# Attention outputs in tiles of 32 columns with sums of key tiles, the maxima's transfers first, the values' bias at the split

## The reference, cut to what matters

```
x = x + attn(layernorm(x))
x = x + ffn(layernorm(x))
attn: Q, K, V = x@Wq.T+bq, x@Wk.T+bk, x@Wv.T+bv; rotary Q, K
      scores = Q K^T / sqrt(32), causal;  out = softmax(scores) @ V;  out @ Wo.T + bo
ffn:  (silu((x@gate.T)*gs) * ((x@up.T)*us)) @ down.T * ds
```

## Time and profile before

| | us |
|---|---|
| median of three runs | 750.68 (748.65 to 753.9) |
| the profiled execution | 749.88 |
| its span, from the first to the last instruction | 748.2 |

### The profile page before, as it was taken

How to read it: one execution, slowest core, us unless ns; L and a number is a source line. 1 busy time by engine, 2 the same in 40 slices (tenths; PEclk the granted TensorE clock), 3 DMA queues, 4 the chain that set the end, 5 groups by cost and what they waited for, 6 DMA issues and landing times.

```text
span 748.2 us, 10633 instructions
## 1 busy us (share of the span) xinstructions
PE 732.0 (98%) x3563; PEld 539.3 (72%) x3563; DVE 443.8 (59%) x1071; ACT 310.9 (42%) x641; POOL 247.7 (33%) x224
## 2 busy tenths in 40 slices
PE   8999999999999999999999999999999999999996
PEld 7887888766656666666666548788788888888885
DVE  6978684897778787777878545853243125114113
ACT  3322231266666666666666662222332232222221
POOL 0816152411114242333324245822232223223223
PEclk9999999999999999999999999999999999999999
DMA  8686469635576667676667356540001001001001
GB/s 280 230 284 232 162 254 309 255 115 160 162 192 172 185 172 194 168 188 164 187 162 187 102 185 225 222 201 1 0 20 38 0 1 56 0 0 56 1 1 59
DMA packets 54318, 104.39 MB, mean 140 GB/s; under 512 B 14820, under 2 KB 18404, under 8 KB 53748
## 3 DMA queue, kind: packets, MB, share of 16 engines
q1 hardware_dynamic: 54264, 103.72, 44.0%
HBM read 69.62 MB, written 38.21 MB: 144 GB/s over the span
## 4 chain that ended last, share of the span: by engine, by line
PE 81%; DVE 6%; issue 5%; DMA 3%; POOL 2%; ACT 1%; SPq 1%; DVEq 0%; POOLq 0%; ACTq 0%
PE ps L1105 32%; PE ps L1244 18%; PE ps L1130 10%; PE ps L1223 10%; PE ps L1320 9%; DMA x_st<-in_x 1%; PE ps L1097 1%; POOL hid_lo L592 1%; DVE xn L786 1%; DVE stats L771 1%; DMA rec_l<-rec_rows 1%; DMA w_st<-in_wk 1%; DMA l_cols<-o_raw 1%; ACT p L683 0%; DVE esin L893 0%
## 5 line engine op out<-in xcount | busy, mean ns | idle before, releaser
L683 ACT ACTIVATE p<-ps 128x384 f32<-128x384 f32 (+3 forms) x384 | 162.0, 489 | 58.0 <-PE ps L1223 57.8
L843 DVE CUSTOM_DVE_ANT_0 masked<-ps,mask_qk 128x512 bf16<-128x512 f32 (+1 forms) x240 | 113.2, 500 | 56.6 <-PE ps L1130 55.7
L1244 PE MATMUL ps<-p,v_slot 128*64 128x512 f32 (+3 forms) x768 | 137.3, 494 | 0.2 <-ACT o_raw L690 0.2
L1223 PE MATMUL ps<-q_st,k_st 99*128 99x384 f32 (+2 forms) x384 | 135.7, 361 | 1.1 <-ACT p L683 1.0
L1056 DVE SCALAR_TENSOR_TENSOR hid<-ps,us_sb,silu 128x512 f32<-128x512 f32 x44 | 33.0, 751 | 165.2 <-PE ps L1105 159.5
L1130 PE MATMUL ps<-k_st,q_st 96*128 96x512 f32 (+2 forms) x384 | 128.9, 357 | 2.0 <-DVE row_max L843 1.7
L592 POOL TENSOR_TENSOR hid_lo<-hid,hid_hi 128x512 fp32r<-128x512 f32 x44 | 56.8, 1290 | 173.0 <-ACT hid_hi L758 173.0
L561 POOL TENSOR_SCALAR_AFFINE_SELECT p<-p 128x512 f32<-128x512 f32 x64 | 40.6, 635 | 209.0 <-ACT p L683 209.0
L1244 PEld LDWEIGHTS ps<-p,v_slot 128*64 128x64 f32 x768 | 50.1, 136 | 74.2 <-issue 62.2
L1130 PEld LDWEIGHTS ps<-k_st,q_st 96*128 96x128 f32 x384 | 72.3, 189 | 29.7 <-DVE row_max L843 14.3
L1223 PEld LDWEIGHTS ps<-q_st,k_st 99*128 99x128 f32 x384 | 72.1, 189 | 16.9 <-issue 6.3
(11 more groups left out here) (117 smaller groups left out, 1080.8 us busy)
## 6 DMA issues: line engine op xcount, KB each, us to landing
qk_scratch<-st_hi SPq DMA_DIRECT2D x32, 512.0 KB, 3.6
q_st<-qk_scratch SPq DMA_DIRECT2D x32, 384.0 KB, 3.8
k_st<-qk_scratch SPq DMA_DIRECT2D x32, 384.0 KB, 4.8
flag_st<-in_ffn SPq DMA_DIRECT2D x32, 264.0 KB, 2.8
ffn_copy<-in_ffn SPq DMA_DIRECT2D x32, 264.0 KB, 3.5
qk_scratch<-st_lo SPq DMA_DIRECT2D x16, 512.0 KB, 3.7
o_T<-o_raw SPq DMA_DIRECT2D x32, 128.0 KB, 4.2
rec_l<-rec_rows SPq DMA_DIRECT2D x32, 128.0 KB, 3.3
```

The costliest lines, as they stand in the source:

```text
L683: act.activation(p32[:, at:at + q0 + w - keep], ps[:, ST_BANK + i % ST_RING, keep - q0:w], ACT.Exp, scale=SCALE).then_inc(exp_done, 1)
L843: ins = dve.tensor_tensor_reduce((masked_a if u < 2 else masked)[:, s_before(i) % 2, col:col + kept], scores, mask_qk[:, 512 - kept:512], ...
L1223: pe.matmul(ps[:, ST_BANK + i % ST_RING, 0:w], k_st[0:K_ALL, slot, kt * P:(kt + 1) * P], q_st[0:K_ALL, slot, q0:q0 + w], start=True, stop= ...
L1244: ins = pe.matmul(ps[VW * a:VW * (a + 1), o_bank(u, half), q0 - 512 * half:512], v_slot[:, slot, kt, :], p32[:, at:at + n], start=(kt == 0 ...
```

## The change

It has these parts.

- Output products: the second half of the queries becomes two quarters (parts 1 and 2, 256 queries each). In them the values, and the rows that held the sums, are separate matmuls of 32 columns, four tiles side by side for a pair. POOL adds the probabilities of key tiles 0 to 3 (`sum_p`, heads 0 to 29), and one product with ones takes that sum. In the rows beside the sums a second set of columns ("w") takes the values' products of some key tiles; they are added later on POOL (`o_w`). The last pair has the old kind of product in quarters (`PV_TAIL`).
- ACT copies three parts out of PSUM for each pair, not two; a pair's move has six transfers, not four.
- SP's step begins with the maxima's rows; the pair's move and the reciprocals' rows come after them.
- The bias of the values is no longer added by POOL, but in `o_hi` and `o_lo`, in four pieces for each tile.
- The weights' test runs in two halves, the output weights are loaded in step 30 and not in stage A, the two small loads for stage C come ahead of the last moves, and POOL's order of the last groups changes. The reciprocals' place on DVE stays; their wait counts six transfers for a pair.

```diff
@@ -94,11 +95,33 @@
 GROUPS = HEADS // 4
 PV_AFTER = ((3, 9), (3, 9))
 TEST_AFTER = (4, 4)
-PV_GROUPS = [[(0, 0), (0, 1), (0, 2), (0, 3)], [(1, 0), (1, 1)], [(1, 2), (1, 3), (1, 7)], [(1, 4), (1, 5), (1, 6)]]
-assert len(PV_GROUPS) == len(PV_AFTER[0]) + len(PV_AFTER[1])
-assert sorted(sum(PV_GROUPS, [])) == [(0, kt) for kt in range(4)] + [(1, kt) for kt in range(KT)]
-PV_HIGH = min(g for g, group in enumerate(PV_GROUPS) if any(2 * kt >= KT for _, kt in group))
-PV_LAST = ((0, 3), PV_GROUPS[-1][-1])
+PV_GROUPS = [
+    (0, [[("vl", 0)], [("vl", 1)], [("vl", 2)], [("vl", 3)]]),
+    (1, [[("v", 0), ("w", 4)], [("v", 1), ("l", None)], [("v", 2), ("l", 4)], [("v", 3), ("l", 5)], [("w", 5)]]),
+    (2, [[("v", 0), ("w", 6)], [("v", 1), ("l", None)], [("v", 2), ("l", 4)]]),
+    (2, [[("v", 3), ("l", 5)], [("v", 4), ("l", 6)], [("v", 5), ("l", 7)], [("w", 7)]]),
+]
+PV_TAIL = [
+    PV_GROUPS[0],
+    (1, [[("vl", kt)] for kt in range(6)]),
+    (2, [[("vl", kt)] for kt in range(4)]),
+    (2, [[("vl", kt)] for kt in range(4, 8)]),
+]
+assert len(PV_GROUPS) == len(PV_TAIL) == len(PV_AFTER[0]) + len(PV_AFTER[1])
+PV_FIRST = {("vl", 0, 0), ("vl", 1, 0), ("vl", 2, 0), ("v", 1, 0), ("w", 1, 4), ("v", 2, 0), ("w", 2, 6)}
+PV_LAST = {("vl", 0, 3), ("vl", 1, 5), ("vl", 2, 7), ("v", 1, 3), ("l", 1, 5), ("w", 1, 5), ("v", 2, 5), ("l", 2, 7), ("w", 2, 7)}
+PARTS = 3
+PART_DONE = (2, 4, 4)
+QW = 256
+
...
 
             def move_pair(u):
 
-                sp.wait_ge(o_evac, 2 * u + 2)
+                sp.wait_ge(o_evac, PARTS * (u + 1))
                 if u % 2 == 0 and u >= 2:
                     sp.wait_ge(l_out, 16 * (u // 2))
                 for a in range(2):
                     t = 2 * u + a
                     rows = slice(t % 4 * D, (t % 4 + 1) * D)
-                    sp.dma_start(o_T[rows, t // 4, :], o_raw[2 * D * a:2 * D * a + D, u % 2, :]).then_inc(o_moved[u % 2], 16)
-                    sp.dma_start(l_cols[:, t % 4, :], o_raw[2 * D * a + D:2 * D * a + D + 1, u % 2, :].rearrange("o (p e) -> o p e", e=KT)).then_inc(o_moved[u % 2], 16)
+                    v_rows, l_rows = slice(VW * a, VW * a + D), slice(VW * a + D, VW * (a + 1))
+                    sp.dma_start(o_T[rows, t // 4, :], o_raw[v_rows, u % 2, 0:S]).then_inc(o_moved[u % 2], 16)
+                    sp.dma_start(l_cols[:, t % 4, :], o_raw[VW * a + D:VW * a + D + 1, u % 2, 0:S].rearrange("o (p e) -> o p e", e=KT)).then_inc(o_moved[u % 2], 16)
+                    sp.dma_start(o_w[t // 4 % 2][rows, :], o_raw[l_rows, u % 2, S:S + 2 * QW]).then_inc(o_moved[u % 2], 16)
+
+            def move_last_pair():
+
+                u = PAIRS - 1
+                sp.wait_ge(o_evac, PARTS * PAIRS)
+                for a in range(2):
+                    row = VW * a + D
+                    sp.dma_start(l_cols[:, 2 + a, :], o_raw[row:row + 1, u % 2, 0:S].rearrange("o (p e) -> o p e", e=KT)).then_inc(o_moved[u % 2], 16)
+                for a in range(2):
+                    sp.dma_start(o_T[(2 + a) * D:(3 + a) * D, GROUPS - 1, :], o_raw[VW * a:VW * a + D, u % 2, 0:S]).then_inc(o_moved[u % 2], 16)
...
             def b_step(t):
+                if t + 1 < HEADS:
+                    load_max(t + 1)
                 if t % 2 == 0 and t >= 4:
                     move_pair((t - 4) // 2)
                 if t % 4 == 3 and t >= 7:
                     store_rec((t - 7) // 4)
-                if t + 1 < HEADS:
-                    load_max(t + 1)
...
+                if t == HEADS - 2:
+                    sp.wait_ge(st_ps, NPC * t)
+                    sp.dma_start(wo_st[:, :, :], wo).then_inc(wo_in, 16)
...
             sp.wait_ge(v_copied, HEADS)
             load_x(xr[:, 0, :, :], 0).then_inc(xr_in[0], 16)
             load_x(xr[:, 1, :, :], 1).then_inc(xr_in[1], 16)
-            move_pair(PAIRS - 2)
-            sp.wait_ge(pv_half[1], PAIRS)
+            sp.wait_ge(pv_part[2], part_done(2, PAIRS - 1))
             sp.dma_start(bo_sb[:, :], bo.partition_broadcast(P)).then_inc(c_in, 16)
             sp.dma_start(ds_sb[:, :], ds.partition_broadcast(P)).then_inc(c_in, 16)
-            move_pair(PAIRS - 1)
+            move_pair(PAIRS - 2)
+            sp.wait_ge(pv_part[2], part_done(2, PAIRS))
+            move_last_pair()
             store_rec(GROUPS - 1)
...
             def scale_group(g):
 
                 pool.wait_ge(rec_in, 64 * (g + 1))
-                pool.tensor_tensor(o_T[:, g, :], o_T[:, g, :], rec_l[:, :], ALU.mult).then_inc(o_scaled, 1)
-                pool.wait_ge(o_scaled, g + 1)
-                pool.tensor_scalar(o_T[:, g, :], o_T[:, g, :], bv_sb[:, g % KC:g % KC + 1], None, ALU.add).then_inc(o_done, 1)
-
-            def mask_p(t):
+                pool.tensor_tensor(o_T[:, g, S // 2:S], o_T[:, g, S // 2:S], o_w[g % 2][:, :], ALU.add).then_inc(o_joined, 1)
+                pool.wait_ge(o_joined, g + 1)
+                pool.tensor_tensor(o_T[:, g, :], o_T[:, g, :], rec_of(g), ALU.mult).then_inc(o_scaled, 1)
...
+            def sum_p(t):
+
+                def second_half(kt):
+                    at = t % SLOTS * P_SIZE + P_OFF[kt] + S // 2 - P * kt
+                    return p32[:, at:at + S // 2]
+
+                total = p_sum[:, t % SUM_SLOTS, :]
+                if t >= SUM_SLOTS:
+                    pool.wait_ge(p_sum_read, 2 * ((t - SUM_SLOTS) // 2 + 1))
+                pool.tensor_tensor(total, second_half(0), second_half(1), ALU.add).then_inc(p_sum_step, 1)
+                pool.wait_ge(p_sum_step, 2 * t + 1)
+                pool.tensor_tensor(total, total, second_half(2), ALU.add).then_inc(p_sum_step, 1)
+                pool.wait_ge(p_sum_step, 2 * t + 2)
+                pool.tensor_tensor(total, total, second_half(3), ALU.add).then_inc(p_summed, 1)
+
...
             for t in range(HEADS):
                 copy_v(t)
                 if t % 4 == 0 and t >= 8:
                     scale_group((t - 8) // 4)
-                mask_p(t)
-
-
-            scale_group(GROUPS - 2)
+                mask_low(t)
+                if t < HEADS - 2:
+                    sum_p(t)
+                mask_high(t)
+
...
+            def evacuate(u, part):
+
+                act.wait_ge(pv_part[part], part_done(part, u + 1))
                 if u >= 2:
-                    act.wait_ge(o_moved[u % 2], 64 * (u // 2))
-                act.copy(o_raw[:, u % 2, half * 512:(half + 1) * 512], ps[:, o_bank(u, half), :]).then_inc(o_evac, 1)
+                    act.wait_ge(o_moved[u % 2], 96 * (u // 2))
+                src = ps[:, o_bank(u, part), :]
+                if part == 0:
+                    act.copy(o_raw[:, u % 2, 0:S // 2], src).then_inc(o_evac, 1)
+                elif u == PAIRS - 1:
+                    act.copy(o_raw[:, u % 2, S // 2 + QW * (part - 1):S // 2 + QW * part], src[:, 0:QW]).then_inc(o_evac, 1)
+                else:
+                    dst = o_raw[:, u % 2, S // 2:S + 2 * QW].rearrange("p (s q c) -> p s q c", s=2, c=QW)
+                    act.copy(dst[:, :, part - 1, :], src.rearrange("p (s c) -> p s c", c=QW)).then_inc(o_evac, 1)
...
                     if i == M_AFTER and t + 1 < HEADS:
                         next_max(t)
                     if t % 2 == 0 and t >= 2 and i == PV_AFTER[0][0]:
-                        evacuate_half((t - 2) // 2, 0)
+                        evacuate((t - 2) // 2, 0)
+                    if t % 2 == 0 and t >= 2 and i == PV_AFTER[0][1]:
+                        evacuate((t - 2) // 2, 1)
                     if t % 2 == 1 and t >= 3 and i == PV_AFTER[1][1]:
-                        evacuate_half((t - 3) // 2, 1)
+                        evacuate((t - 3) // 2, 2)
...
-                act.copy(oT_hi[:, :, j * P:(j + 1) * P], o_T[:, b * KC:(b + 1) * KC, cols]).then_inc(o_hi_done, 1)
-
-            evacuate_half(PAIRS - 1, 0)
+                for kc in range(KC):
+                    ins = act.activation(oT_hi[:, kc, j * P:(j + 1) * P], o_T[:, b * KC + kc, cols], ACT.Identity, bias=bv_sb[:, kc:kc + 1])
+                ins.then_inc(o_hi_done, 1)
...
+                for half in range(2):
+                    if t == 0 and half == 0:
+                        dve.wait_ge(flag_init, 1)
+                    else:
+                        dve.wait_ge(flag_done, 2 * t + half)
+                    cols = slice(half * FFN_PIECE // 2, (half + 1) * FFN_PIECE // 2)
+                    dve.scalar_tensor_tensor(out=flag_bits[:, :], in0=flag_st[:, cols].bitcast(I32), scalar=(1 << 12) - 1,
+                                             in1=flag_bits[:, :], op0=ALU.bitwise_and, op1=ALU.bitwise_or).then_inc(flag_done, 1)
...
-                dve.tensor_tensor(oT_lo[:, :, tile], o_T[:, b * KC:(b + 1) * KC, cols], oT_hi[:, :, tile].bitcast(F32), ALU.subtract).then_inc(o_lo_done, 1)
+                for kc in range(KC):
+                    ins = dve.scalar_tensor_tensor(out=oT_lo[:, kc, tile], in0=o_T[:, b * KC + kc, cols], scalar=bv_sb[:, kc:kc + 1],
```

(54 more changed lines are left out.)

100 lines of the change are left out of this document (63 added, 37 removed).

## The result

The changed kernel takes 766.75 us (median of four runs, 766.05 to 768.25) where the kernel before takes 750.18 beside it; the ratio is 1.0215, with a 95% interval of 1.0185 to 1.0245. I had said 748.9, with 762 as the upper end. The profiled execution has a span of 764.6 us, 16.4 more than the 748.2 before. One of the later executions, the longest of e12 at 786.82 us, ran in a slower state than the others and is left out of its time and ratio.

A forecast was written before the change was run, and what follows sets the result against it. PE was taken to bound the kernel: 749.88 - 18.6 (fewer columns) + 16.8 (waits for reciprocals) = 748.1, and 0.8 for the runs' median gave 748.9 us. Own range 735 to 757; 732 to 762 held at about 0.83.

The forecast's parts named there:

- What bounds the kernel: Whole kernel: PE, busy 98% of the span, sets the pace; in the attention the other engines wait for it.
- Part one: Output groups 2 and 3 of odd steps: fewer PE columns save 1.26 us a pair, -18.6 us in all.
- Rival B: Output products: four tiles do not overlap, 4.2 us a pair more than forecast, giving 802 us; chance 0.08.
- rival C: Small output tiles: PE's issue of records, not columns, sets the pace, giving 755 to 763 us; chance 0.06.
- Part two: SP's queue, maxima first: late moves delay DVE's reciprocals, so PE stands 2.8 us in six steps, +16.8 us.
- the landing: Time a pair's move takes to arrive on SP's queue: put at 4.2 us, with bounds of 2.1 to 5.1.
- Part three: POOL's sums of key tiles in the attention, 3.6 us a head: hidden, cost 0; without cover up to 1 us a step.
- Part four: Values' bias moved into four small ACT and DVE operations a tile, about 1.1 us each, and the stage's end: cost 0.
- the tail: End of the attention stage, with moved loads and a late move: no net change, 2 us either way.
- the chain of the last sums: Late chain that met PE at 471.46 after a 1.2 us gap: assumed to meet it there again, within 2 us.
- A: Attention: reciprocals do not hold PE, as the move lands in about 2 us or the wait vanishes: 732 us; chance 0.14.
- D: Attention: six PE idles of 2.5 us lower the granted clock, costing 16 us and giving 765; chance 0.10.

The follow-up runs named there:

- e12: e11 with DVE's test of the weights after entry 9 in odd steps, not after entry 4: 771.62 us, ratio 1.0254.
- e7: Changed kernel with POOL's sums of key tiles left out, a one-column fill in their place: 764.12 us.
- e13: e4 with DVE's test of the weights left out, a one-column fill for each half: 752.94 us.
- e2: Changed kernel with SP's old queue order, the pair's move and reciprocals' rows ahead of the maxima's rows: 757.72 us.
- e9: Changed kernel with POOL's old order: seventh group scaled ahead of the first additions of the output bias: 767.37 us.
- e11: Changed kernel with e8's joined edits, its bias loads moved to the end of steps with t % 4 = 0, plus e9's order: 746.08 us, ratio 0.9921.
- e4: Changed kernel with DVE's reciprocals one place later, after entry 3 of the next step: 759.46 us.
- e6: Changed kernel with the values' bias on POOL again, one operation a tile, and the output weights loaded after the reciprocals' store: 758.71 us.
- e8: Changed kernel with the bias added in POOL's copy of the values, e4's reciprocals, one operation a tile, output weights loaded after the store: 763.74 us.
- e15: e11 with POOL scaling a group two steps later, in steps with t % 4 = 2: 755.44 us, ratio 1.0046.

## Why the prediction was wrong, step by step

**What bounds the kernel**: right, PE did, with 0.1 us a pair to spare. What I did not ask is how far behind PE the next engine stands at each place. A pair's shortest times fell by 1.22 us, and PE's waits for the queue's transfers and for DVE's test, none of which stood in the trace of before, came out.

**Part one**: right. 1.22 us a pair against 1.26; groups at 1.43 and 1.44 against 1.46. Rival B (tiles taking turns) and rival C (a price for each record) fall: group 2 has 24 records and group 3 has 28, in the same time, which is that of their columns.

**Part two**: the mechanism right, the size wrong. DVE's reciprocals do wait in these steps, for the last transfer of the move, and PE behind them. The term that was mis-sized is the landing. The queue of step 18, DVE, and the landing of transfers out of `o_raw` (min/median/max), for the earlier trace rows:

```profile
315.49 1.33 SPq L454 DMA_DIRECT2D q_st<-neg_T  x2
316.86 0.56 SPq L465 DMA_DIRECT2D o_T<-o_raw  x1
...
320.00 0.60 SPq L467 DMA_DIRECT2D o_w<-o_raw  x1
```

```profile
322.08 0.35 DVE L1062 RECIPROCAL l_cols<-l_cols 128x32 f32<-128x32 f32 x1 [0.95 <-DMA o_w<-o_raw]
```

```profile
DMA to landing us min/median/max: 2.0/2.3/7.8
```

I took 4.2 us for the landing, the median of before, where the move went together with two loads of a head; alone it takes 2.1 to 2.3, the lower bound that I had named. So DVE waits 0.95 us and not 3.0, and PE loses some 0.75 us in such a step (4.5 in six) and not 2.8. The 12 us that I put in excess there were made up, for 8.6 us, by two waits that I had not seen: the keys (the same edit: the move pushes the weights' loads against the keys' load, which lands in 6.3 us in place of 5.0 in the stretch from 331 to 352) and the bank behind the test. That the sum of the stage came out right was luck: two errors of opposite sign.

**Part three**: "Cost 0; without cover up to 1 us a step" was nearly right: by e7 the sums cost 0.16 us a pair at the bank behind the test, 2.2 us in fourteen pairs. The cover that I named, DVE's idle time, exists, but not at the place where the test stands: e13 says that the test itself costs 0.24 us a pair (17.75 to 17.51) as soon as the odd step is shorter; the wait behind it goes from 3.5 to 0.2 us in twelve pairs.

**Part four**: this is the step that failed: "Cost 0" for the pieces, and 2 us for the tail, where C1 grew by 17.6 us. I costed DVE's four pieces by the shortest row of their kind, 1.1 us a tile, and set it against PE's 2.8. That row is of 8 partitions, one of its two inputs lies in PSUM (`ps`), and no POOL operation runs beside it. The trace of before had the warning in the earlier trace rows: the remainder of a tile is 979 ns in the mean, and I never asked why, though I had asked it of the test, in part three, one paragraph earlier. In the rows above each piece waits for a POOL operation of its own, whatever its own 0.34 us, so four pieces pay that wait four times. The Trainium skill, page "SBUF — State Buffer", section "Who interferes with whom", has the rule: a VectorE instruction with two inputs in SBUF (the memory that these tiles lie in) contends with a GpSimd instruction that reads SBUF, and it calls the ports that they share "an exclusive lock". The trace agrees: 0.34 us alone, 6.37 us for four beside POOL's row of operations, 20.7 us in place of 34.9 for all pieces when POOL has almost no additions. In the same part I let the chain of the last sums "meet at the same place, with 2 us either way". It did not, since three moves that I had listed stand ahead of that chain: the output weights (4.9 us alone), POOL's order (2.0 alone, 6.0 once the other two are gone), and the late move of pair 13. That one I had sized at 5 to 7 us and then given no cost; e2 shows the queue's tail 6.1 us earlier without it, and C1 6.3 us shorter.

**The rivals**: A had the size of the landing right, but the wait did not vanish, and 732 was far off. D's mechanism showed. In the changed kernel's trace the clock did not fall after the waits in the attention, but around the 6.95 us of idle in C1, for about 1.6 us; in e9, with the same attention, it fell behind a wait of 1.23 us, half the idle that I had put as its condition, for about 3.4 us. No rival had the projection in it, so the range could not reach it: I gave the tail 2 us for four edits in it.

What stays open: how the 6.0 us that the pieces and POOL's order give only together come about, when the clock falls behind a wait of 1 to 2 us and when it does not, and why e11's pairs are 0.2 us longer than e4's (the copy with two inputs takes 0.73 us on POOL where the plain copy took 0.39 to 0.60, and six loads were added among the pairs; the two weren't tried apart, and 0.2 us is within chance here).

## What to carry to other kernels

Before an operation is cut into pieces on VectorE, look at what GpSimd does beside it, and cost a piece by the mean beside GpSimd's work and not by the shortest row. When the bounding engine is made faster, each wait that it hid comes out as soon as the saving is larger than its slack; list these slacks first, place by place. On one in-order queue a transfer that waits, or a large one ahead of a small store, is a price for everything behind it, also where both of them look idle. And a wait of TensorE can cost more than its own length: look at the granted clock behind it.

## What the runs showed of the hardware

Four operations of VectorE with two inputs in memory, 0.34 us each alone, took 6.37 us beside a row of GpSimd operations; each ended 0.14 to 0.15 us behind one of these. A store of 16 KB behind a load of 1 MB took 7.2 us, and about 2 with the load behind it. Four tiles of 32 columns cost what their columns cost: 768 columns took 1.43 us in 24 records and 1.44 in 28. At waits of TensorE of 1.0 to 3.2 us, or just behind them, the granted clock fell to 0.50 at fifteen places of the attention in six of the runs (e2, e6, e8, e9, e12, e15); at others of this size, 1.05 us in the changed kernel and 1.42 in e11, it stayed at 1.00.
